# An AdaLN-conditioned mixture-of-experts layer on one core: the opening, the first body's exponentials and the placing of the merge rounds are rearranged

## The reference, cut to what matters

```python
q_emb = relu(q @ W3 + b3)                       # q = cond_1024, 128 x 256
x1 = (n * v + sum(v, axis=1)) * q_emb           # v = x, n = 64
h  = relu(x1 @ W2 + b2)                         # what the FFN sees
logits = h @ gate_w.T                           # 64 experts
scores = softmax(logits); top 6 of each token
slots: each expert takes its first 64 tokens in order of token number
y_e = silu(buf @ w_gate) * (buf @ w_up) @ w_down   # per expert
out = x + sum of the 6 weighted expert rows + silu(h @ sw_gate) * (h @ sw_up) @ sw_down
```

## Time and profile before

| | us |
|---|---|
| median of three runs | 1251.76 (1250.82 to 1252.1) |
| the profiled execution's own time | 1252.05 |
| its span, first to last instruction | 1250.3 |
| PE busy, of the span | 1229.3 (98%) |
| DVE busy | 709.3 (57%) |
| ACT busy | 352.7 (28%) |

### The profile page before, as it was taken

The page is one execution under the profiler, slowest core; times in us unless marked ns, Lnnn a source line. Parts: engine busy times, 40 slices in busy tenths (PEclk is TensorE's granted clock), DMA queues, the critical chain, the costliest instruction groups (busy, mean ns, idle before and its releaser), DMA issues.

```text
span 1250.3 us, 15818 instructions
## 1 busy us (share of the span) xinstructions
PE 1229.3 (98%) x5976; PEld 913.0 (73%) x5976; DVE 709.3 (57%) x1369; ACT 352.7 (28%) x663; POOL 143.8 (12%) x118
## 2 busy tenths in 40 slices
PE   6999999999999999999999999999999999999998
PEld 6877778888888888888776676676666666666666
DVE  6889898989888898877423232332322322322322
ACT  3655243433424343343121120211201211111110
POOL 0000000000000000000012222221222222122220
PEclk8999999999999999999999999999999999999999
DMA  9945437264543627157667987989799798798852
GB/s 189 232 115 146 99 89 189 71 149 93 153 106 94 171 80 171 28 152 252 212 227 242 311 298 232 328 285 275 269 276 308 267 303 287 261 302 285 276 131 76
DMA packets 157180, 250.90 MB, mean 201 GB/s; under 512 B 21488, under 2 KB 92272, under 8 KB 155952
## 3 DMA queue, kind: packets, MB, share of 16 engines
q1 hardware_dynamic: 143888, 223.66, 56.8%
q0 software_dynamic: 11488, 25.17, 10.0%
q10 hardware_dynamic: 1728, 1.05, 0.3%
HBM read 197.14 MB, written 61.10 MB: 207 GB/s over the span
## 4 chain that ended last, share of the span: by engine, by line
PE 89%; DVE 5%; ACT 2%; issue 1%; DMA 1%; SPq 1%; ACTq 0%; DVEq 0%
PE bank L1326 21%; PE bank L1328 21%; PE bank L1327 21%; PE bank L1525 12%; PE bank L1548 7%; PE bank L1508 1%; PE bank L1438 1%; PE bank L1437 1%; PE bank L1372 1%; PE bank L1375 1%; PE bank L1534 1%; DMA x<-in_x_dram 1%; SPq L381 1%; DVE prod L903 0%; DMA outst<-in_x_dram 0%
## 5 line engine op out<-in xcount | busy, mean ns | idle before, releaser
L1326 PE MATMUL bank<-hh,gu 128*128 128x512 f32 x704 | 280.9, 399 | 2.9 <-DVE prod L903 2.1
L1328 PE MATMUL bank<-hh,gu 128*128 128x512 f32 x704 | 274.5, 390 | 0.0
L1327 PE MATMUL bank<-hl,gu 128*128 128x512 f32 x704 | 274.4, 390 | 0.0
L1326 PEld LDWEIGHTS bank<-hh,gu 128*128 128x128 f32 x704 | 132.5, 188 | 43.0 <-issue 14.0
L903 DVE TENSOR_TENSOR prod<-bank,prod 128x512 f32<-128x512 f32 x96 | 66.1, 688 | 155.7 <-PE bank L1328 137.4
L1328 PEld LDWEIGHTS bank<-hh,gu 128*128 128x128 f32 x704 | 132.1, 188 | 28.4
L1327 PEld LDWEIGHTS bank<-hl,gu 128*128 128x128 f32 x704 | 132.3, 188 | 25.4
L606 ACT ACTIVATE ah<-prod 128x512 fp32r<-128x512 f32 x96 | 60.5, 631 | 291.6 <-DVE prod L903 291.6
L1326 PE MATMUL bank<-sdh,ah 128*128 128x512 f32 x320 | 126.8, 396 | 0.0
L1327 PE MATMUL bank<-sdl,ah 128*128 128x512 f32 x320 | 124.6, 390 | 0.0
L1328 PE MATMUL bank<-sdh,al 128*128 128x512 f32 x320 | 124.6, 389 | 0.0
(11 more groups left out here) (119 smaller groups left out, 1629.3 us busy)
## 6 DMA issues: line engine op xcount, KB each, us to landing
wg<-in_L_ffn_w_gate_dram SPq DMA_DIRECT2D x64, 704.0 KB, 9.3
wu<-in_L_ffn_w_up_dram SPq DMA_DIRECT2D x64, 704.0 KB, 11.1
wd<-in_L_ffn_w_down_dram SPq DMA_DIRECT2D x64, 512.0 KB, 5.3
table<-hrow SPq DMA_DIRECT2D x64, 256.0 KB, 4.4
x<-in_x_dram SPq DMA_DIRECT2D x60, 256.0 KB, 7.0
wd<-in_L_ffn_w_down_dram SPq DMA_DIRECT2D x64, 192.0 KB, 5.9
out_dram<-outst SPq DMA_DIRECT2D x36, 256.0 KB, 4.5
outst<-in_x_dram SPq DMA_DIRECT2D x32, 256.0 KB, 3.8
```

What stands on the lines that cost most here:

```text
L1326: nc.tensor.matmul(o, st_h, mv_h, start=first_mm, stop=False)
L1327: nc.tensor.matmul(o, st_h, mv_l, start=False, stop=False)
L1328: return nc.tensor.matmul(o, st_l, mv_h, start=False, stop=last_mm)
```

## The change

It moves instructions and adds some transposes; no other arithmetic is touched.

- PE: `keep_clock(n)` issues n transposes of the identity: 6 ahead of the condition's transposes, 14 ahead of the products with W3, 56 instead of 32 behind them.
- DVE and ACT, opening: the first two pieces of W2 are split ahead of x's first half, the other two right behind it; `x_turn(0,1)` comes after all that.
- Body 0: `exp_scores(a)` leaves its place between `split_a(v,1)` and `silu(v,2)` on ACT and stands where `exp_scores(b)` stood, behind `take_cond(c,0)`; `exp_scores(b)` now comes ahead of `take_cond(c,3)`. On DVE `score(a)` moves behind `split_h(c,0)` and `score(b)` behind `take_down(v,0)`. Since z of chunk 0 must live longer, it gets memory of its own (`z_first`, in the place of `w3p`). SP's store of chunk 0's scores moves behind the load of x chunk 4.
- Merging: body 1 does 10 rounds instead of 12, body 2 does 11 instead of 10, and body 3 does 9 instead of 8. `take_ranks(2)` on ACT moves behind `split_a(v,3)`.

```diff
+        z_first = Place(w3p_at)("z_first", [P, J, E])
...
                     load_xr(i, 1)
                     keep_x(0)
-                    store_scores(a)
                     store_rows(b)
                 if d + 1 < NCH:
                     load_x(d + 1)
+                if i == 0:
+                    store_scores(a)
                 store_scores(b)
...
+            split_piece(0, slice(0, 2))
             split_xm(0, 0)
-            split_piece(0)
+            split_piece(0, slice(2, 4))
...
                 split_a(v, 1)
-                if i == 0:
-                    exp_scores(a)
                 silu(v, 2)
...
-                if 1 < i < ND - 1:
+                if 2 < i < ND - 1:
                     take_ranks(i)
                 silu(v, 3)
...
+                if i == 2:
+                    take_ranks(i)
                 silu(v, 4)
...
                     take_cond(c, 0)
-                    exp_scores(b)
+                    exp_scores(a if i == 0 else b)
                     take_cond(c, 1)
                     take_cond(c, 2)
+                    if i == 0:
+                        exp_scores(b)
                     take_cond(c, 3)
...
-                wait(dve, s.exp_ready, n)
+                wait(dve, s.exp_ready, n if n > 1 else 0)
...
                     if i == 2:
-                        merge(1, 6)
+                        merge(1, 4)
+                    if i == 3:
+                        merge(2, 7)
-                    m = [(0, 6), (0, 7)] + [(1, r) for r in range(6)] if i == 1 else [(i, r) for r in range(NR)]
+                    m = [(0, 6), (0, 7), (1, 0), (1, 1), (1, 2), (1, 3)] if i == 1 else \
+                        [(1, 7)] + [(2, r) for r in range(7)] if i == 2 else [(i, r) for r in range(NR)]
...
                     if i == 2:
-                        merge(1, 7)
+                        merge(1, 5)
...
-                    if i == 1:
-                        merge(0, 5)
+                    if i in (1, 2):
+                        merge(i - 1, 4 + i)
...
-            split_xm(0, 0)
-            split_piece(0, slice(0, 2))
+            split_piece(0, slice(0, 2))
+            split_xm(0, 0)
+            split_piece(0, slice(2, 4))
+            x_turn(0, 1)
             x_sum(0, 1)
-            split_piece(0, slice(2, 4))
...
+            def keep_clock(n):
+                for _ in range(n):
+                    nc.tensor.transpose(bank[7][:, 0:P], ident[:, :], ident[:, :])
...
             pe.wait_ge(s.condT_ready, 1)
+            keep_clock(14)
             pe.wait_ge(s.w3_ready, QC)
...
-            for _ in range(32):
-                nc.tensor.transpose(bank[7][:, 0:P], ident[:, :], ident[:, :])
+            keep_clock(56)
```

More of the change, by code:

```diff
@@ L110, in adaln_moe_ffn_kernel @@
         xml = keep("xml", [P, KC, CH], F32R)
+        w3p_at = keep.at
         w3p = keep("w3p", [P, QC, D])
@@ L327, in cond_bank, with z_of @@
             return bank[(5, 6, 1, 2)[oc] if n == 0 else (3, 4, 5, 6)[oc] if n == 1 else (4, 5, 6, 4)[oc]]
+        def z_of(n):
+            return z_first if n == 0 else z
         def lraw_bank(n):
@@ L648, in exp_scores @@
                 for j in range(J):
-                    op = nc.scalar.activation(ez[:, j, :], z[:, j, :], ACT.Exp, accum_out=ssum[:, j:j + 1])
+                    op = nc.scalar.activation(ez[:, j, :], z_of(n)[:, j, :], ACT.Exp, accum_out=ssum[:, j:j + 1])
                 op.then_inc(s.exp_ready, 1)
@@ L1028, in body, with top, drop @@
                     if i == 2:
-                        merge(1, 6)
-                    m = [(0, 6), (0, 7)] + [(1, r) for r in range(6)] if i == 1 else [(i, r) for r in range(NR)]
+                        merge(1, 4)
[3 more added lines that the diff above has]
+                        [(1, 7)] + [(2, r) for r in range(7)] if i == 2 else [(i, r) for r in range(NR)]
+                    def top(k):
+                        if k < len(m):
+                            merge_top(*m[k])
+                    def drop(k):
+                        if k < len(m):
+                            merge_drop(*m[k])
                     route(b)
@@ L1047, in body @@
                     product(v, 2)
-                    if i == 1:
-                        merge(0, 5)
+                    if i in (1, 2):
+                        merge(i - 1, 4 + i)
                     x_scale(c, 1)
                     split_a(v, 2)
-                    merge_top(*m[0])
+                    top(0)
                     x_turn(d, 0)
-                    merge_drop(*m[0])
+                    drop(0)
                     split_xm(c, 1)
                     product(v, 3)
-                    merge_top(*m[1])
+                    top(1)
                     split_a(v, 3)
-                    merge_drop(*m[1])
+                    drop(1)
                     x_sum(d, 0)
                     product(v, 4)
-                    merge_top(*m[2])
+                    top(2)
                     x_pair(d, 0)
@@ L1065, in body @@
                     split_a(v, 4)
-                    merge_drop(*m[2])
+                    drop(2)
                     x_scale(d, 0)
                     product(v, 5)
-                    merge_top(*m[3])
+                    top(3)
                     split_a(v, 5)
-                    merge_drop(*m[3])
+                    drop(3)
                     x_turn(d, 1)
@@ L1081, in body @@
                     x_scale(d, 1)
-                    merge_top(*m[4])
+                    top(4)
                     split_xm(d, 0)
                     take_down(v, 0)
-                    merge_drop(*m[4])
+                    drop(4)
                     take_rows(c, 0)
-                    merge_top(*m[5])
+                    top(5)
                     split_xm(d, 1)
-                    merge_drop(*m[5])
+                    drop(5)
                     take_rows(c, 1)
                     take_down(v, 1)
-                    merge_top(*m[6])
+                    top(6)
                     take_rows(c, 2)
-                    merge_drop(*m[6])
+                    drop(6)
                     take_rows(c, 3)
-                    merge_top(*m[7])
+                    top(7)
                     take_down(v, 2)
-                    merge_drop(*m[7])
+                    drop(7)
             def first_half():
@@ L1114, in first_half @@
                 x_pair(c, 1)
-                score(a)
                 x_shift(c, 1)
@@ L1133, in first_half @@
                 split_piece(8)
-                score(b)
                 split_h(c, 0)
+                score(a)
                 split_h(c, 1)
@@ L1149, in first_half @@
                 take_down(v, 0)
+                score(b)
                 split_xm(d, 1)
@@ L1439, in down_tile @@
                 op.then_inc(s.down_filled, 1)
+            def keep_clock(n):
+                for _ in range(n):
+                    nc.tensor.transpose(bank[7][:, 0:P], ident[:, :], ident[:, :])
             pe.wait_ge(s.consts_ident, 2)
+            keep_clock(6)
             pe.wait_ge(s.cond_loaded, 16)
```

4 lines of the change are left out of this document (2 added, 2 removed).

## The result

The changed kernel is slower: 1254.03 us against 1251.19 us, medians of 12 runs each (1253.02 to 1255.05 and 1250.59 to 1252.25). The ratio is 1.0023, with a 95% interval of 1.0015 to 1.0031, so the loss is 2.8 us, from 1.9 to 3.9. It was predicted to gain 0.5 us, and 1254.03 lies above the range. (The forecast of 1251.3 started from a median of three runs, 1251.76.

A forecast was written before the change was run, and what follows sets the result against it. PE's last idle time, ending at 158.76, was taken to follow x rows landing through SP; of 2.2 us gained by 108 us, 0.5 passes: 1252.05 to 1251.55, less 0.29 for the median, 1251.3 us; range 1249.2 to 1253.2.

The forecast's parts named there:

- Where the end is decided: PE is busy from 160 us on, so only moving the gate/up tile at 158.76 moves the end.
- case 5: New idle time behind 160 us from moved merge rounds or take_ranks(2): 1 to 4 us lost, 1252.5 to 1255.5, chance 0.05.
- Opening: Start of kernel: earlier first product, q late by 0.35 us; worth 0.7 us, from 1.05 gained to 0.3 lost.
- So the tile of 34.63 starts at 33.9: PE's tile after chunk 0's second half: DVE 0.3 ahead and its 0.40 us wait for ACT gone.
- Case 4: Clock low in the opening, transposes not holding it or falling in the new 2.7 us pause: 1251.8 to 1252.5, chance 0.06.
- the row: Profile row of the granted clock in the opening: it fell over 3 us after 32 transposes, suggesting they held it up.
- Body 0: PE's waits at 72.12 and 83.82 go, 1.7 us; with the opening, PE is 2.2 us early at 108 us.
- the step that failed: SP, end of body 0: store_out(0,0) issued at 109.4, landing in 2.4; rows' stores begin at 112.2, 0.5 us early.
- The bounds: Landing of store_out(0,0): in 2.0 gives 0.9 us early; 1 MB wholly in front, 3.1 us, gives 2.2 late.
- Merging: Merge rounds moved between bodies 1, 2 and 3: cost 0; without DVE's cover in body 2, up to 1 us.
- case 3: SP's burst of h delays store_out(0,0), landing 0.5 us later than taken: likely 1252.3 to 1253.3, bound 1254.0, chance 0.12.

The follow-up runs named there:

- the scores alone: Kernel before with only the moved exponentials, the later score(a) and score(b) and SP's moved scores store: +0.67 us (1251.98 against 1251.31).
- the scores and merging: Changed kernel without its opening part, measured against the kernel before: +1.02 us (1252.24; ratio 1.0009).

## Why the prediction was wrong, step by step

**Where the end is decided: right.** The tile at 158.76, plus a constant, is the end. In the changed kernel and in each experiment whose `take_down(0,3)` waits for x rows, that tile starts 27.2 to 27.3 us behind `take_down(0,3)`. No idle time came up behind 160 us; case 5 did not occur.

**Opening.** The products with W3 started at 9.41 (9.4), q was 0.49 late (0.35), the first product came at 18.23 (18.1), the pause ended at 26.94 (26.65). Then the step "So the tile of 34.63 starts at 33.9" failed: 35.15. It took the full pace for granted behind the new pause. Case 4 named that fall, priced it at 0.4 lost and gave it 0.06; it measured 0.5 lost in the trace (from the restart to the next tile 8.2 us, and 7.3 where the clock held), and the traces of six of the seven kernels with the opening and an open pause of 2.3 us show it. The 0.06 was too little: the one case of a fallen clock in the trace of before also followed an idle time, and a kernel that makes a new pause of nearly 3 us should have had it near even odds. On the other half of that case the row was right. The Trainium skill's page "TensorE: Matmul & The Clock Gate", section "Part 4: PE-mode transpose", says that a transpose doesn't count as PE being busy in the same way; here PE made 56 transposes up to 18.3 us and then worked at full pace, and 18 of them in the pause kept the granted clock at 1.00 in three traces. The measurement decides for the row.

**Body 0: right.** The waits at 72.12 and 83.82 are gone, and with the scores alone `take_down(0,0)` started 2.4 us earlier. In the changed kernel PE was 1.2 early near 109 us, not 2.2: 0.5 lost in the opening in place of 0.7 gained makes the difference.

**SP: the step that failed.** "It lands behind 1 MB of h: I take 2.4 instead of 2.0." It measured 3.15 to 3.25 in five traces without the packet and 3.56 in the trace of the changed kernel. The bounds were right (2.0 and 5.1); the choice was too near the lower one. The bytes could have been added up, and would have misled all the same: the scores, h and the output are 1.44 MB; at the best rate, 391 GB/s, that is 3.7 us, and a store alone began to move 0.8 us behind its issue and was seen as landed 0.4 us behind its last byte. With the scores and merging (scores issued at 107.01) that gives 111.9, a landing of 2.4 to 2.5 us. In the first view of DMA above the bytes move from 107.9 to 112.1: for the first 0.7 us at 236 to 240 GB/s, while the scores go (608 packets of the burst are under 512 B), and not at 391 without a break afterwards either, 343 GB/s in the mean. The load then leaves at 112.70. So the best rate was the wrong one to take: the burst's mean was some 12% below it, it started later than taken, and every part of that falls on the last in the queue. With 3.2 for the landing the rows' stores would have been summed 0.3 us late in place of 0.5 early, near what the scores alone show (112.86 against 112.72). The other 1.0 us, an issue at 110.42 and not at 109.4, is the slip of `take_down(0,0)`, which ended at 107.4 and not at 106.4, and that is the opening's 1.2 us again. So the rows' stores, summed for 112.2, began at 114.36: 1.0 of these 2.2 us is the opening's and 1.2 the landing's, of which 0.8 is the burst and 0.3 the engine that was behind. The rest of the way was as taken, 1.89 later at `take_down(0,3)` for 1.64 later here; by the spread of that way over the traces (17.6 to 19.7 us) this close agreement is in part luck.

**What was in no step.** The 44 transposes were costed by their time on PE and found free there. Their other effect is that every later packet of what seem to be PE's instructions comes earlier, and one came to stand in or at the end of the burst on which the end hangs. Where it stood inside (four traces) the landing went from 3.2 to 4.6 us, more than twice the surplus over 2.0. In the medians 50 transposes cost 1.8 us with the old order of the opening; how much of that is the packet isn't shown. Together: 0.7 to 1.0 for the store behind h, 1.8 for the longer stream, some 0.3 to 0.7 for the fallen clock, up to 0.5 given back by the new order; the sum of 2.3 to 3.5 holds the 2.8, though each term is known to about one microsecond only, so this is no proof that the list is complete.

**Merging: right**, at 0. DVE's fourth product of body 2 moved from 229.29 to 230.99, less than the 1.90 by which everything had moved, and PE didn't wait for it.

**The cases.** Cases 3 and 4 came true together, and case 3 at its stated condition, a landing 0.5 us later than taken: it was 1.2 later. Its likely price, 1252.3 to 1253.3, was too low; the measured 1254.03 is at its bound. They had 0.18 between them, as if they excluded each other; they add up. That the loss would be over 0.2% had 0.05.

**What stays open.** How the packet holds an engine back: in four traces one engine is 1.5 us late with the packet, of 0.9 us, inside the burst, and in two, the changed kernel's among them, one engine is 0.3 late though the packet starts only when the store's last one has ended. Which of the executions without a trace had it where. How much of the 1.8 us it accounts for, since in the one pair of traces that isolates the transposes 1.4 us of landing left only 0.4 at `take_down(0,3)`, and since the kernel with 16 transposes fewer is 1.95 above before with its packet out of the way. That the packets carry PE's instructions is inferred: they move with the number of PE's instructions. Why the clock held behind one of seven equal pauses isn't known either.

## What to carry to other kernels

When an edit puts one wait in front of others on an in-order DMA queue, list what stood behind it and add up the bytes that will now be in the engines at once: a small store whose landing releases the next load pays for all of them. Issue the store on the critical path first, and the megabytes that nobody awaits behind it; here that was worth 3.5 us of 1254, more than the 2.2 by which the rearrangement was to make PE early. And no instruction is free because its engine is idle: dummies keep the clock, but they shift what comes after, so judge them by the time of the whole kernel and look for a new pause of PE before it costs the clock.

## What the runs showed of the hardware

- The landing of a 256 KB store took 2.0 us on empty engines and 3.15 to 3.25 us behind 1 MB issued just ahead on the same queue, with the 16 engines at 343 GB/s in the mean over the burst.
- With one packet of 16 KB of another queue within such a burst, a single DMA engine ended some 1.5 us behind the other fifteen (four traces), and the store's landing came 1.4 us later. Without it no engine was more than 0.1 late (five traces).
- The granted clock fell 1.2 us after PE had come back from a pause of 2.33 us, not in the pause (0.3 to 1.2 us after it in six traces), and stayed at half for 3.4 us under a full load of products. Behind an equal pause in another kernel it didn't fall. Behind the pause of 1.8 us near 127 us it fell in two traces of four, with 10 and 34 transposes more than the changed kernel.
- With 18 transposes of the identity in the same pause the clock stayed at 1.00, in all three traces that have them.
